# Second attention of a two-layer decoder: another order of GpSimd's work within a tile, with the keys' sum one tile later

## What is computed

```python
x = x + attention1(layernorm(x))          # 16 heads of 16, causal
x = x + experts(layernorm(x))             # top 2 of 8, per output feature
# second attention, on h = layernorm(x), 16 heads, not causal
kv_c, q_lat = h @ d_kv_w.T + d_kv_b, h @ d_q_w.T + d_q_b        # 64 latent columns each
k_c, q_c = linear(kv_c, u_k), linear(q_lat, u_q)                # 128 per head
k_r, q_r = rope(linear(kv_c, qr)), rope(linear(q_lat, qr))      # 64 rotary columns per head
scores = concat(q_c, q_r) @ concat(k_c, k_r).T / sqrt(192)
ctx = softmax(scores) @ linear(kv_c, u_v)
x = x + ctx @ out_w.T + out_b
x = x + ffn(layernorm(x))                 # Walsh-Hadamard transforms, silu(gate) * up, down
```

## Time and profile before

| what | value |
|---|---|
| median of 3 runs | 2500.35 us (2495.98 to 2503.32) |
| the profiled execution | 2502.4 us, its span in the trace 2501.1 us |
| granted TensorE clock, mean | 0.977 |
| busy: TensorE, VectorE, ScalarE, GpSimd | 2217.8, 2149.0, 1866.5, 1074.6 us |
| VectorE busy in 1000 to 1500 us | 490.25 of 500 us |
| GpSimd busy in 1000 to 1500 us | 311.74 of 500 us |
| second attention's tiles | from about 850 to about 2312 us |

### The profile page before, as it was taken

The page is one execution under the profiler, slowest core; times in us unless marked ns, Lnnn a source line. Parts: engine busy times, 40 slices in busy tenths (PEclk is TensorE's granted clock), DMA queues, the critical chain, the costliest instruction groups (busy, mean ns, idle before and its releaser), DMA issues.

```text
span 2501.1 us, 50461 instructions
## 1 busy us (share of the span) xinstructions
PE 2217.8 (89%) x18456; PEld 1581.9 (63%) x18544; DVE 2149.0 (86%) x3182; ACT 1866.5 (75%) x2640; POOL 1074.6 (43%) x1480
## 2 busy tenths in 40 slices
PE   4888888869998699999999999999999999988899
PEld 2444444445555467777777777777767767766687
DVE  6888888858896899999999999999999999988421
ACT  4777777646666588888888888888888888877411
POOL 3311211101213475665665656656656657622200
PEclk9999999989999899999999999999999999999899
DMA  3000000041000399999999999999999999999100
GB/s 127 1 2 1 2 1 1 2 95 21 1 1 1 57 181 190 193 192 192 189 194 192 198 187 192 197 185 193 197 191 189 196 191 189 203 197 197 38 17 17
DMA packets 1119317, 300.67 MB, mean 120 GB/s; under 512 B 1107232, under 2 KB 1116416, under 8 KB 1118208
## 3 DMA queue, kind: packets, MB, share of 16 engines
q1 hardware_dynamic: 1116224, 295.21, 67.9%
q10 hardware_dynamic: 2848, 2.23, 0.3%
HBM read 18.45 MB, written 2.10 MB: 8 GB/s over the span
## 4 chain that ended last, share of the span: by engine, by line
DVE 28%; PE 20%; issue 9%; ACT 5%; DMA 4%; SPq 0%; DVEq 0%; POOL 0%; ACTq 0%; POOLq 0%
DVE parts L1601 13%; DVE lows L1585 12%; DMA partsT<-parts 4%; PE psS L1536 3%; PE psOb L1456 3%; PE psS L1439 2%; ACT parts L1785 2%; PE psS L1441 2%; PE psS L1440 2%; PE psOb L1492 1%; ACT prob L1775 1%; PE psOb L1457 1%; PE psOb L1556 1%; PE psPb L1556 1%; DVE shift L1593 1%
## 5 line engine op out<-in xcount | busy, mean ns | idle before, releaser
L1775 ACT ACTIVATE prob<-psS,shift 128x1024 f32<-128x1024 f32 x512 | 574.7, 1122 | 169.0 <-DVE shift L1593 158.8
L1601 DVE TENSOR_TENSOR parts<-prob,parts 128x1024 f16<-128x1024 f32 x512 | 660.9, 1291 | 23.5 <-ACT parts L1785 20.0
L1585 DVE TENSOR_REDUCE lows<-psS 128x1 f32<-128x1024 f32 x512 | 621.3, 1214 | 3.6 <-PE psS L1441 3.1
L1785 ACT CAST parts<-prob 128x1024 f16<-128x1024 f32 x512 | 536.6, 1048 | 22.4 <-DMA partsT<-parts 18.6
L1439 PE MATMUL psS<-k_hi,q_lo 128*128 128x512 f32 x1024 | 447.6, 437 | 103.1 <-ACT prob L1775 95.7
L1456 PEld LDWEIGHTS psOb<-kv,partsT 128*128 128x128 f16 x4096 | 357.0, 97 | 93.8 <-issue 75.8
L1456 PE MATMUL psOb<-kv,partsT 128*128 128x130 f16 x4096 | 397.4, 221 | 15.2 <-DMA partsT<-parts 15.0
L1441 PE MATMUL psS<-k_hi,q_hi 128*128 128x512 f32 x1024 | 406.7, 397 | 0.0
L1440 PE MATMUL psS<-k_lo,q_hi 128*128 128x512 f32 x1024 | 404.3, 395 | 0.0
L1457 PE MATMUL psOb<-kv,partsT 128*128 128x66 f16 x4096 | 387.2, 193 | 0.0
L1457 PEld LDWEIGHTS psOb<-kv,partsT 128*128 128x128 f16 x4096 | 360.5, 98 | 1.0 <-issue 1.0
(11 more groups left out here) (292 smaller groups left out, 3920.3 us busy)
## 6 DMA issues: line engine op xcount, KB each, us to landing
partsT<-parts SPq DMA_TRANSPOSE x512, 4.8
ef<-in_ewT SPq DMA_DIRECT2D x1, 2048.0 KB, 9.9
rf<-in_rwT SPq DMA_DIRECT2D x1, 2048.0 KB, 10.0
outw_s<-in_outwT SPq DMA_DIRECT2D x1, 2048.0 KB, 8.4
trig<-in_trig SPq DMA_DIRECT2D x2, 1024.0 KB, 11.0
out_x<-ot SPq DMA_DIRECT2D x16, 128.0 KB, 1.7
wug<-in_wupT SPq DMA_DIRECT2D x4, 256.0 KB, 3.7
wug<-in_wgateT SPq DMA_DIRECT2D x4, 256.0 KB, 3.7
```

Of the source, the lines that this page charges most:

```text
L1585: dve.tensor_reduce(lows[:, n % 2, g:g + 1], psS[:, (2 * n + g) % 3, :], AX_X, ALU.min).then_inc(half_min, 1)
L1601: dve.tensor_tensor(parts[:, s, 1, :], prob[:, g, :], parts[:, s, 0, :], ALU.subtract).then_inc(low_done, 1)
L1775: act.activation(prob[:, g, :], psS[:, (2 * n + g) % 3, :], ACT.Exp, bias=shift[:, n % 2:n % 2 + 1], scale=-1.0).then_inc(exp_done, 1)
L1785: act.copy(parts[:, s, 0, :], prob[:, g, :]).then_inc(high_done, 1)
```

## The change

GpSimd alone is rewritten, with the same operations in number and shape. `add_up` now makes one sum per call. In an iteration n GpSimd first waits for the first subtraction of tile n (2n + 1); then, in tiles i = 3, 6, 9, 12, it makes the keys' sum; then the split, then `add_bias` or `add` and `take_weights`. After that it waits for the second subtraction (2n + 2) and does one long operation: the queries' sum at i = 2, 5, 8, 11, the queries' rest at 3, 6, 9, 12, the keys' rest at 4, 7, 10, 13. The other engines' instructions keep their order.

```diff
--- before.py
+++ after.py
@@ -1878,16 +1878,16 @@
                 pool.tensor_copy(beta_h[latent, :], beta[latent, head:head + 1]).then_inc(weights_in, 1)
                 pool.wait_ge(weights_in, done + 1)
 
-            def add_up(head, j):
-                c = 4 * head + j
-                pool.wait_ge(rotated, 2 * c + 2)
-                if c:
-                    pool.wait_ge(rests_done, sums(head, j))
-                if (head, j) == (1, 0):
-                    pool.wait_ge(keys_rested, NB)
-                for side, (out_rows, rows) in enumerate(((whole, rotary), (whole_k, latent))[:2 if head else 1]):
-                    pool.tensor_tensor(out_rows[rotary, :], rot[0][rows, :], rot[1][rows, :], ALU.add).then_inc(added_up, 1)
-                    pool.wait_ge(added_up, sums(head, j) + side + 1)
+            def add_up(head, j, keys):
+                if not keys:
+                    pool.wait_ge(rotated, 2 * (4 * head + j) + 2)
+                    if 4 * head + j:
+                        pool.wait_ge(rests_done, sums(head, j))
+                    if (head, j) == (1, 0):
+                        pool.wait_ge(keys_rested, NB)
+                out_rows, rows = (whole_k, latent) if keys else (whole, rotary)
+                pool.tensor_tensor(out_rows[rotary, :], rot[0][rows, :], rot[1][rows, :], ALU.add).then_inc(added_up, 1)
+                pool.wait_ge(added_up, sums(head, j) + 1 + keys)
 
             def rest_queries(head, j, halves_scored):
                 slot = q_slot(head, j)
@@ -1947,7 +1947,7 @@
             pool.wait_ge(filled, 1)
             take_weights(0)
             for j in range(NB):
-                add_up(0, j)
+                add_up(0, j, False)
                 rest_queries(0, j, 0)
             take_weights(1)
             for n in range(TILES + 3):
@@ -1955,21 +1955,23 @@
                 j, turn = divmod(i - 2, 3)
                 ahead = n < TILES and head < NH
                 if n < TILES:
-                    pool.wait_ge(low_done, 2 * n)
+                    pool.wait_ge(low_done, 2 * n + 1)
+                if ahead and 2 <= i <= 13 and turn == 1:
+                    add_up(head, j, True)
+                split(n - 3)
                 if n < NT:
                     add_bias(n)
                 add(n - LATER - 1)
                 if ahead and i == 14 and head + 1 < NH:
                     take_weights(head + 1)
                 if n < TILES:
-                    pool.wait_ge(low_done, 2 * n + 1)
+                    pool.wait_ge(low_done, 2 * n + 2)
                 if ahead and 2 <= i <= 13 and turn == 0:
-                    add_up(head, j)
+                    add_up(head, j, False)
                 if ahead and 2 <= i <= 13 and turn == 1:
                     rest_queries(head, j, 2 * (n + 1))
                 if ahead and 2 <= i <= 13 and turn == 2:
                     rest_keys(head, j)
-                split(n - 3)
             for i in range(2 * len(halvings)):
                 butterfly(i)
 
```

## The result

The changed kernel takes 2554.61 us (median of 4, 2554.0 to 2556.2) against 2499.86 (median of 4, 2495.98 to 2503.32): a ratio of 1.0227, 95% interval 1.0215 to 1.0239. It is slower by 54.75 us; 2552 was forecast, with a range of 2508 to 2576.

What follows compares the result with a forecast made beforehand. VectorE was taken to bound the kernel, so what lengthens its list lengthens the tile. Added waits of 92.5 us less 41 gave +51.5 us, forecast 2552 us against the median 2500.35, range 2508 to 2576.

Steps and rivals of the forecast that it cites:

- Rules A and B: Subtraction issued during a GpSimd operation waits until its end less 0.12 us; conversely GpSimd ends its length less 0.14 behind.
- Part 1: Subtractions of line 1601: nearly all waiting for GpSimd operations already running goes, -41 us.
- Part 2: Behind the second subtraction: the long GpSimd operation overlaps the next subtraction, costing 0.25 us, twelve times a head in 15 heads.
- the bound with 0.22 us: Long operation starting 0.22 us behind the subtraction's end: 0.07 more on some 150 of them, +11 us.
- Part 3: Tiles i = 3, 6, 9: keys' sum delays the rotate 0.20 us, split's end costs 0.16; together 0.36, 45 times.
- the branch that I took with 0.03 us to spare: Tiles i = 3, 6, 9: second subtraction due at E0 + 2.23, after the split's third operation starts at E0 + 2.20.
- Parts 4 and 5: Late additions hold ScalarE's copy: 1.04 us at even heads' i = 3, 6, rest 0.77 at 9; tile 12 0.93 even, 1.62 odd.
- Only the stretches count: Long operations collide, but rotate, part and tile 12 find slack: +4 us, 2504, no change; chance 0.08.
- The second stretch is free: Long operation behind the second subtraction costs nothing if over, or yielding, by E1 + 1.06 + 0.12: -25 us, 2475; chance 0.11.
- The "worse" one: Even heads: queries' rest issued just ahead of the subtraction blocks it 1.16 us; 2567 to 2587 us, chance of worse 0.09.

## Why the prediction was right

**The bound.** VectorE's list sets the tile, and what lengthens it lengthens the kernel: held, in every experiment. From the first subtraction's start (tile 0) to the last one's (tile 255) the changed kernel takes 1514.8 us and the one before 1456.9: 57.8 more; the profiled spans differ by 53.8. The other 4 lie ahead of the first subtraction, where the change touches nothing: it starts at 853.9 us in the kernel before and at 850.0 in the changed one, and between 848.1 and 852.5 in the nine other traces.

**Rules A and B** held to 0.01 us at both ends (1.46 for a predicted 1.46; 0.60 behind the subtraction for the addition).

**Part 1**, the 41 us that go: held in the main. No subtraction of the changed kernel waits for the keys' sum. Additions still reach into the second one at i = 13 and 14 of odd heads (1.66 us, medians), which I hadn't named; there VectorE then waits for ScalarE that much less, and the tiles are as long as before. The same holds for tile 13 in the kernel before: its second subtraction takes 1.41 us, but the wait for ScalarE behind it is 0.20 us shorter for that in odd heads and 0.12 in even ones. So some 2 of the 41 us never cost time, and couldn't be gained.

**Part 2** was 0.25 and is 0.24. The choice of the earlier start was right: the bound with 0.22 us would have given 0.32. Issuing the operation inside the subtraction at i = 2 to 11 took 27.2 us away: the cause is shown, and that is most of what this part costs.

**Part 3** was 0.36 and is 0.35, in other portions: the rotate is 0.24 late instead of 0.20, the split costs 0.11 instead of 0.16. The subtraction did come behind the split's last operation (1533.60 and 1533.53), the branch that I took with 0.03 us to spare. What I had said the profile would show, VectorE idling 0.2 us at line 1569, the list of waits shows with 2.2 us in 14 places only. The rows have it in all 45, at 0.13 to 0.16 us each (here the shift ends at 1532.71 and the rotate starts at 1532.85); the list names only the longest. And even 0.14 is too little, since in the kernel before the rotate is recorded as starting 0.08 us ahead of the shift's end. The starts, 1.29 and 1.52 behind the subtraction, are the better reading.

**Parts 4 and 5** held: 1.09 for 1.04, 0.78 for 0.77, 0.92 for 0.93, 1.68 for 1.62. Two buffers for `part` show that ScalarE's wait is a cause. VectorE's wait for ScalarE did grow, from 20.0 to 49.1 us; the 23.5 us that I gave for it before is all of VectorE's idle time ahead of the subtraction.

**What failed.** The sum left out tile 15 of odd heads. There ScalarE waits for an addition as well (GpSimd's late addition, ScalarE and VectorE in head 3):

```profile
1226.46 0.75 POOL L1933 TENSOR_TENSOR x<-x,part 128x256 f32<-128x256 f32 x1
```
```profile
1227.30 0.47 ACT L1809 ACTIVATE part<-psOb,kv_unit 128x256 f32<-128x256 f32 x1 [1.19 <-POOL x L1933]
```
```profile
1228.74 1.23 DVE L1601 TENSOR_TENSOR parts<-prob,parts 128x1024 f16<-128x1024 f32 x1 [1.71 <-ACT parts L1785]
```

The weights of tile 14 now wait for its first subtraction and stand behind its split and addition. They start 2.03 us behind that subtraction's end, where they started 1.02 us ahead of it, and end 0.94 us behind the first subtraction of tile 15, where they ended 1.83 ahead of it (medians). So the split and the addition of tile 15 come late, ScalarE waits 1.19 us before it can copy `part`, and the subtraction waits 1.71 for ScalarE, 0.41 before. I had looked at tile 14 only for collisions of the weights themselves and not for what they push ahead of them. At 7 x 1.30 that is 9.1 us missing. Tile 13 was charged too much (0.25 for 0.12 and 0.20, 1.4 us), since VectorE waits for ScalarE there anyway. With these the sum is 51.5 + 9.1 - 1.4 = 59 us for the attention, and 61 with the 2 us of part 1; 57.8 are found. Counted by head, the odd ones from 1 to 13 lose 4.5 us each and the even ones from 2 to 12 3.8 to 4.1, but head 14 loses only 1.0. There the kernel before has waits that the changed one doesn't have: before 2166.50 ScalarE waits 0.82 us for the DMA that transposes the parts, and VectorE 0.68 for ScalarE. On the pages ScalarE's wait for that DMA is 18.6 us in the kernel before and 12.0 in the changed one. That makes up for some 3 us, which the sum has at nothing; why the waits go isn't shown. The sum for the attention was some 6 us short all the same. That 2552 came within 3 us of 2554.6 is partly luck: the 4 us ahead of the attention went the other way.

**The rivals.** "Only the stretches count" (2504) falls with the two buffers: `part` and tile 12 found no slack. "The second stretch is free" (2475) was wrong as the change is written, yet its condition was the useful thing in it: an operation that is held in the subtraction, and so is over 0.28 us sooner, does cost nothing. The "worse" one, the queries' rest issued a hair before the subtraction, occurs only in tile 12 of even heads, where it was in the sum.

## What to carry to other kernels

Where two engines exclude each other, the room between two of one engine's operations has to be measured against the other's operation plus its release: a 1.28 us operation that starts 0.14 us after a release doesn't fit 1.06 us of room, whatever lies in that room. Issue the operation while the excluding one still runs: its wait is then the lock's, not a semaphore's, and it was over 0.28 us sooner here. But not just ahead of the excluding one: issued 0.23 us before a subtraction, it held that up by 0.92 us. And follow each moved operation to the buffer behind it, and to what it pushes into the next tiles: the addition itself held VectorE up by 0.5 us, but through the one buffer and ScalarE it cost up to 1.7 us at a time.

## What the runs showed of the hardware

A GpSimd operation that is held ends 1.14 us behind the subtraction though it takes 1.28 alone, and a held subtraction loses 0.12 us less than the overlap. Both look as if part of an instruction ran before it needs the lock; no run shows what that part is. The lock went by the order of issue, not to the engine that had it: a subtraction issued at 1521.60, while one sum runs, goes ahead of the second sum issued at 1522.06. And an operation over 128 rows of 512 numbers takes 1.277 us on GpSimd, over 64 rows 1.269 to 1.291 (means of the four long operations of the kernel before).
